# A transformer decoder block: cross attention and the stages before and after it, one after the other or in one order of gaps

## The chip, the cores and the metric

One core of one Trainium2 chip runs the program. The metric is the device time of one execution in microseconds (us), the median of several runs. The profile is one execution of the kernel before, recorded by the hardware profiler.

## The reference

A decoder block in float32: 4 batches of 1024 tokens, width 256, 16 heads of 16, a context of 154 tokens per batch, a feed-forward width of 1024. Cut to what is computed:

```python
nx = _ln(x, ln1_scale, ln1_bias)
q, k, v = heads(nx @ W_qkv)
x = x + merge(_attend(q, k, v, causal)) @ W_self_out
nx = _ln(x, ln2_scale, ln2_bias)
q = heads(nx @ W_q)
k, v = heads(encoder_output @ W_kv)
x = x + merge(_attend(q, k, v, None)) @ W_cross_out
nx = _ln(x, ln3_scale, ln3_bias)
return x + relu(nx @ W1 + b1) @ W2 + b2
```

## The kernel before, in words

The program is written engine by engine, each with its own fixed order; semaphores join them. SyncE (SP) issues every DMA, in one order. There are five stages, one behind the other.

- **A, the first stage** (`dense_a`): normalize x, q, k and v of self attention, and k and v of the context; parts go to DRAM.
- **SA, self attention** (`attention(SA, ...)`): 16 *windows*, v = 0 to 15. A window is four heads of one batch and has 12 *steps*: one block of 128 keys against a half of 512 queries (less on the diagonal). A step has four scores (`scores`, L765, TensorE (PE), 64 rows of the array in use), four exponentials (ScalarE (ACT), L1015) and the sum with the values (`weigh`, L784, array split in 32 columns). Before the scores of a window come the row maxima of its queries: `max_tile` (PE, L653) and VectorE's (DVE) reduction (L1123), two windows ahead; `turn` (L674), `negate` and `rows` put them as rows into the stack of queries.
- **C, the middle stage** (`dense_c`), for n = 0 to 7 (four batches times two halves of 512 tokens): `project_c` (output of self attention times W_self_out, L818), the sum with x, moments, normalize, `transposes` (L622), and the queries of cross attention (`project`, L627). The first n are begun in SA's last two windows (`ahead_c`), and the first maxima of XA run inside C.
- **XA, cross attention** (`attention(XA, ...)`): 16 windows of 4 steps, against 154 keys. Scores rotate over three banks, maxima over two pairs of banks; weights of the softmax have 16 slots in `probs`, and the sum is taken two steps behind the scores.
- **E, the last stage** (`dense_e`), for n = 0 to 7: `project_e` (W_cross_out), sum, moments, normalize, `transposes`, eight hidden tiles (the products of L635 to L637, bank to ReLU on ACT to a high part on DVE, L1349, to a low part on GpSimd (POOL), L1533), and the second product of the feed-forward. Every product there is three matmuls, high and low parts. In PE's order, `project_e` of the next n and its transposes stand between hidden tiles and result, and inside the result, of this one:

```python
for i in range(2):
    pe.wait_ge(y_done, 2 + 2 * n + i - 1)
    for t in range(2 * i, 2 * i + 2):
        ...
    last.then_inc(f_ready, 1)
    if i == 0 and (hf == 0 or more):
        transposes(E, n + 1, 1 - hf, 2)
```

Between the five scores' places of a step lies what else PE does: the lists `units_at`, `weigh_at` and `turn_at` of each `Attention` count these places (five to a step, `5 * s + i`). Call them *gaps*: 60 in a window of SA, 20 in one of XA. In SA's last two windows and in XA's, `ahead` adds the first steps of the stage that follows.

## Time and profile before

| | us |
|---|---|
| median of 3 runs | 1096.2 |
| runs | 1088.33 to 1098.66 |
| the profiled execution | 1099.86 |
| its span, first to last instruction | 1098.1 |
| PE busy | 1008.1 |
| DVE, ACT, POOL busy | 784.1, 612.4, 331.5 |
| mean granted clock of PE | 0.950 |

The span is what the trace covers; 1.8 us of the profiled execution lie around it. A granted clock of 1.00 is 2.4 GHz and of 0.50 is 1.2 GHz; a mean between them is a stretch with both.

### The profile page before, as it was taken

Reading aid. Unit: us, or ns where it says so; the run is one execution under the profiler, and the core shown is the slowest. Engines: PE = TensorE matmul, PEld = TensorE weight load, DVE = VectorE, ACT = ScalarE, POOL = GpSimd, SP = SyncE. Lnnn points to the kernel's source line nnn. Section 1 sums busy time; section 2 is a strip of 40 time slices with the busy share of each in tenths; the row PEclk is TensorE's granted clock in tenths of the full one; section 3 lists DMA queues with packets and bytes.
Section 4 is the critical chain, followed back from the end, with each engine's and each line's share of the span. In section 5 each row is a group of like instructions: output and inputs, shape, how many; then the busy total and the mean of one; then the engine's idle time right before and its main releaser. Section 6 shows DMA issues by size and latency. Waiting matters only on the chain.

```text
span 1098.1 us, 19967 instructions
## 1 busy us (share of the span) xinstructions
PE 1008.1 (92%) x7632; PEld 632.4 (58%) x7632; DVE 784.1 (71%) x1154; ACT 612.4 (56%) x1310; POOL 331.5 (30%) x516
## 2 busy tenths in 40 slices
PE   3968889999999999999999886999998899999997
PEld 3855655555555555555443553444443588888886
DVE  5746677999999999999422575788886855656561
ACT  4623327777777777777654222788887433323221
POOL 8311103323233222322332110011112554545453
PEclk9969999999999999999895997899999899999998
DMA  6885676353535444344015993444542111111100
GB/s 184 295 246 157 188 209 131 60 112 69 112 69 108 68 98 90 70 90 165 21 58 135 286 325 111 94 114 105 123 120 74 50 46 59 58 58 58 39 20 20
DMA packets 78639, 123.47 MB, mean 112 GB/s; under 512 B 11057, under 2 KB 52305, under 8 KB 73553
## 3 DMA queue, kind: packets, MB, share of 16 engines
q1 hardware_dynamic: 78544, 122.21, 43.0%
q8 instruction: 60, 0.98, 0.4%
q14 instruction: 35, 0.28, 0.1%
HBM read 71.96 MB, written 49.17 MB: 110 GB/s over the span
## 4 chain that ended last, share of the span: by engine, by line
PE 78%; DVE 11%; DMA 3%; issue 2%; POOL 2%; ACT 2%; SPq 2%; POOLq 0%; ACTq 0%; DVEq 0%
PE bank L784 18%; PE bank L765 17%; PE bank L653 11%; PE bank L635 8%; DVE mx L1123 8%; PE bank L636 7%; PE bank L637 7%; PE bank L818 2%; PE bank L661 2%; PE bank L627 2%; PE bank L622 1%; ACT probs L1015 1%; DMA vst_mem<-self_ctx 1%; DMA k_st<-k_parts 1%; SPq L417 1%
## 5 line engine op out<-in xcount | busy, mean ns | idle before, releaser
L1015 ACT ACTIVATE probs<-bank 128x512 f32<-128x512 f32 (+3 forms) x1024 | 457.2, 521 | 147.6 <-PE bank L765 141.9
L1123 DVE TENSOR_REDUCE mx<-bank 128x2 f32<-128x1024 f32 (+5 forms) x416 | 435.1, 1084 | 72.9 <-PE bank L653 35.4
L765 PE MATMUL bank<-q_st,k_st 64*128 64x512 f32 (+3 forms) x1024 | 302.3, 439 | 11.7 <-ACT probs L1015 7.5
L765 PEld LDWEIGHTS bank<-q_st,k_st 64*128 64x128 f32 x1024 | 141.9, 189 | 205.2 <-ACT probs L1015 179.6
L653 PE MATMUL bank<-k_st,q_st 62*128 62x154 f32 (+4 forms) x1280 | 229.0, 353 | 31.2 <-DVE mx L1123 20.1
L784 PE MATMUL bank<-probs,nx_mem 128*32 128x512 f32 (+3 forms) x2048 | 239.1, 545 | 0.2
L653 PEld LDWEIGHTS bank<-k_st,q_st 62*128 62x128 f32 x1280 | 145.9, 191 | 77.5 <-DVE mx L1123 58.3
L1454 POOL TENSOR_SCALAR_AFFINE_SELECT probs<-probs 128x256 f32<-128x256 f32 x256 | 103.9, 407 | 226.6 <-ACT probs L1015 226.3
L1533 POOL TENSOR_TENSOR hT_lo<-hT,hT_hi 128x512 fp32r<-128x512 f32 x64 | 93.1, 1475 | 91.9 <-DVE hT_hi L1349 91.9
L1463 POOL TENSOR_TENSOR oN<-oT,rs 128x256 f32<-128x256 f32 x64 | 40.6, 635 | 231.6 <-DVE rs L1207 231.6
L635 PE MATMUL bank<-nxT_lo,hT_hi 128*128 128x256 f32 x256 | 77.6, 303 | 17.7 <-issue 13.7
L936 ACT CAST probs<-bank 128x512 fp32r<-128x512 f32 x48 | 28.2, 587 | 106.1 <-PE bank L627 58.9
L1202 DVE STREAM_TRANSPOSE oT<-bank 128x512 f32<-128x512 f32 x64 | 45.7, 714 | 55.8 <-PE bank L784 55.4
L929 ACT ACTIVATE nxT<-bank,lnb_sb,lns_sb 128x512 f32<-128x512 f32 x48 | 35.0, 778 | 88.5 <-PE bank L622 88.5
L661 PE MATMUL bank<-below,eye 64*128 64x64 bf16 (+1 forms) x1024 | 82.7, 210 | 0.0
L1062 ACT ACTIVATE hT<-bank,b_sb 128x512 f32<-128x512 f32 x64 | 44.2, 690 | 68.8 <-PE bank L637 67.7
L1349 DVE CAST hT_hi<-hT 128x512 fp32r<-128x512 f32 x64 | 60.9, 965 | 26.8 <-ACT hT L1062 26.1
L636 PE MATMUL bank<-nxT_hi,hT_lo 128*128 128x256 f32 x256 | 76.1, 297 | 0.0
L637 PE MATMUL bank<-nxT_hi,hT_hi 128*128 128x256 f32 x256 | 76.0, 297 | 0.0
L784 PEld LDWEIGHTS bank<-probs,nx_mem 128*32 128x32 f32 x2048 | 42.6, 109 | 57.4 <-issue 37.1
L635 PEld LDWEIGHTS bank<-nxT_lo,hT_hi 128*128 128x128 f32 x256 | 53.0, 207 | 19.3 <-issue 19.3
L636 PEld LDWEIGHTS bank<-nxT_hi,hT_lo 128*128 128x128 f32 x256 | 53.2, 208 | 0.0
(119 smaller groups left out, 1260.6 us busy)
## 6 DMA issues: line engine op xcount, KB each, us to landing
xt<-in_x_dram SPq DMA_DIRECT2D x16, 512.0 KB, 5.9
q_parts<-probs SPq DMA_DIRECT2D x16, 512.0 KB, 6.7
k_parts<-probs SPq DMA_DIRECT2D x16, 512.0 KB, 4.0
q_st<-q_parts SPq DMA_DIRECT2D x32, 256.0 KB, 4.8
k_st<-k_parts SPq DMA_DIRECT2D x32, 256.0 KB, 6.6
qx_parts<-probs SPq DMA_DIRECT2D x16, 512.0 KB, 7.4
q_st<-qx_parts SPq DMA_DIRECT2D x32, 256.0 KB, 4.7
v_aug<-vst_mem SPq DMA_DIRECT2D x8, 544.0 KB, 4.4
```

Of the source, the lines that this page charges most:

```text
L635: pe.matmul(dst, a_hi, b_lo, start=(j == 0), stop=False)
L636: pe.matmul(dst, a_lo, b_hi, start=False, stop=False)
L637: last = pe.matmul(dst, a_hi, b_hi, start=False, stop=(j == len(terms) - 1))
L653: last = pe.matmul(banks[:, j, keys * y:keys * y + keys], q_st[w][h0:h0 + KROWS, i, P * qb:P * qb + P], keys_of(a, v0)[h0:h0 + KROWS, i, k ...
L661: last = pe.matmul(banks[:, j, end - width:end], eye[h0:h0 + HALF, e0:e0 + P], below[h0:h0 + HALF, 0:width], start=False, stop=width == HALF)
L765: pe.matmul(bank[:, m, 0:n], keys_of(a, v0)[rows, i // 2, P * kb:P * kb + P], q_st[w][rows, i // 2, lo:lo + n], start=True, stop=True).the ...
L784: last = pe.matmul(bank[32 * i:32 * i + 32, a.acc[hf % a.AB], lo - HF * hf:lo - HF * hf + n], v_cur[w // 2][:, col:col + 32], probs[:, pt, ...
L1015: act.activation(probs[:, use % NPT, 0:n], bank[:, a.s_banks[use % a.SB], 0:n], ACT.Exp, scale=SCALE).then_inc(a.exp_done, 1)
L1123: dve.tensor_reduce(mx[:, par, part].rearrange("p (j y) -> p j y", j=2)[:, :, blocks.start:blocks[-1] + 1:blocks.step], banks[:, :, 0:len( ...
L1349: dve.tensor_copy(hT_hi[:, f, :], hT[:, f % HRING, :]).then_inc(h_hi, 1)
L1454: pool.affine_select(out=tri, in_=tri, compare_op=ALU.is_ge, fill=0.0, base=0, pattern=[[0, 2], [1, P]], channel_multiplier=-1).then_inc(a ...
L1533: pool.tensor_tensor(hT_lo[:, f, :], hT[:, f % HRING, :], hT_hi[:, f, :].bitcast(F32), ALU.subtract).then_inc(h_lo, 1)
```

## The change

Stages C, XA and E are no longer one behind the other. One count of gaps runs through them, `at`, from -120 (SA's last two windows) over 0 to 319 (XA's 16 windows) to 418. Each engine walks the same count and does at each gap what the tables name: `C_PROJECT`, `C_TURN`, `C_PRODUCT` (gaps of each n), and for E the offsets `E_...` from `E_FROM[n]` = 101 + 40 n, so that one n of E takes two windows of XA. At a gap, PE does in this order: the sum of XA with its values (offset 3 of each step, now one step behind), `turn`, a unit of maxima, a score, and what stands `behind`: at most one piece of C or E.

So that all of it fits: every product of C and E goes through two banks in turn (`g_bank`, banks 6 and 7, ordered by `g_order`); XA keeps three score banks, has one accumulator as before, and one pair of banks for maxima in the place of two; XA's weights have 8 slots in the place of 16; its stacks of queries are three and not four, loaded in gap 1 of the window two before the one that uses them; its stacks of keys hold a whole batch and are two. The ring of hidden tiles before their split (`hT`) has two buffers, not four; the high part of a hidden tile is made by ACT, not by DVE; the weights of C and E are split by POOL in 9 pieces in windows 4 to 12 of SA, not by DVE and ACT before E. The rows of W1 and W2 are loaded in window 2 of SA. C's DRAM copy of x + attention and XA's queries remain DRAM round trips. The keys of the context are stored by four DMAs per batch in the place of two.

In the order of PE, between the transposes of an n of E (offset -3) and its first hidden tile (+1) lie four gaps; the hidden tiles stand at +1, +3 to +15, the result at +22, +24, +31 and +33, and `project_e` at -13 and -12.

```diff
+        probs_x, hT_hi = sb("probs_x", [P, NPT - FC, HF]), sb("hT_hi", [P, FC, HF], F32R)
...
+        late_st = sb("late_st", [P, 3, 2 * L], F32R)
+        q_st = [sb(f"q_st{w}", [P, 2, L], F32R) for w in range(3)] + [late_st[:, 1].rearrange("p (i t) -> p i t", i=2)]
+        k_st = [sb(f"k_st{w}", [P, 2, L], F32R) for w in range(2)] + [
+            late_st[:, w].rearrange("p (i t) -> p i t", i=2) for w in (0, 2)]
+        nxT_hi, nxT_lo = (late_st[:, w].rearrange("p (h k t) -> p h k t", h=2, k=KC) for w in (1, 2))
+        hT_lo = late_st[:, 0:2].rearrange("p a (f t) -> p (a f) t", t=HF)
+        cn_hi, cn_lo = (late_st[:, 2].rearrange("p (s k t) -> p s k t", s=2, k=KC)[:, i] for i in range(2))
+        wqx_sb = sb("wqx_sb", [P, KC, D])
...
+        w2_hi = sb("w2_hi", [P, FC, D], F32R)
+        parts_c = sb("parts_c", [P, 2, NPART, HF], F32R)
+        hT = [hT_0, sb("hT_1", [P, HF])]
...
-        XA = Attention("X", False, LX, 2, qx_parts, kx_parts, vx_aug, cross_ctx, [0, 1, 4], [5], [(2, 3), (6, 7)],
-                       units_at=(0, 8, 9, 11, 15, 17), turn_at=4, weigh_at=(1, 0, 3, 2),
-                       sums_at=(5, 1), invert_at=(5, 2), back_at=(6, 5), divide_at=(3, 1))
+        XA = Attention("X", False, LX, 2, qx_parts, kx_parts, vx_aug, cross_ctx, [0, 1, 2], [3], [(4, 5)], 1, NPT // 2, 3,
+                       units_at=(7, 9, 12, 14, 17, 19), turn_at=1, weigh_at=(3, 3, 3, 3),
+                       sums_at=(14, 4), invert_at=(15, 5), back_at=(18, 8), divide_at=(16, 6))
...
+        XG = 5 * XA.NS
+        X_END = 4 * B * XG
+        LAST_SELF = -2 * 5 * SA.NS
+        C_PROJECT = ((-115, -114), (-99, -98), (0, 1), (15, 16), (62, 63), (82, 83), (143, 145), (166, 170))
+        C_TURN = (-101, -85, 8, 23, 70, 92, 158, 180)
+        C_PRODUCT = ((-97, -96), (-81, -80), (11, 12), (26, 27), (73, 74), (94, 95), (160, 161), (183, 187))
+        C_LOAD = (None, None, -77, -65, 25, 72, 98, 160)
+        C_SUM, C_DEV, C_NORM, C_SCALE, C_HIGH, C_LOW, C_STORE = 1, 2, 4, 1, 1, 2, 3
+        E_FROM = tuple(5 * XG + 1 + 2 * XG * n for n in range(2 * B))
+        E_HIGH, E_LOW, E_PROJECT, E_SUM, E_DEV, E_BIAS, E_NORM = -16, -15, (-13, -12), (-12, -11), -10, -9, -7
+        E_TURN, E_SCALE, E_TOKENS, E_REST = -3, -2, -1, 0
+        E_FIRST, E_SECOND, E_ADD = (1, 3, 5, 7, 9, 11, 13, 15), (22, 24, 31, 33), (25, 34)
+        END = E_FROM[2 * B - 1] + E_ADD[1] + 3
+
+        EARLY_X = {**{-56 + 4 * n: (0, n) for n in range(XA.MT)}, **{-29 + 4 * n: (1, n) for n in range(XA.MT)}}
+        EARLY_TURN = -33
+
+        def e_at(n, r):
+            return E_FROM[n] + r
...
+        g_order = []
+        for at in range(LAST_SELF, END):
+            for n in range(2 * B):
+                g_order += [("C", "o", n, i) for i in range(2) if at == C_PROJECT[n][i]]
+                g_order += [("C", "t", n, k) for k in range(KC) if at == C_TURN[n]]
+                g_order += [("C", "q", n, c) for c in range(2) if at == C_PRODUCT[n][c]]
+            for n in range(2 * B):
+                g_order += [("E", "o", n, i) for i in range(2) if at == e_at(n, E_PROJECT[i])]
+                g_order += [("E", "t", n, k) for k in range(KC) if at == e_at(n, E_TURN)]
+                g_order += [("E", "h", n, f) for f in range(FC) if at == e_at(n, E_FIRST[f])]
+                g_order += [("E", "y", n, i) for i in range(2) if at == e_at(n, E_SECOND[2 * i])]
...
+        def g_bank(u):
+            return bank[:, 6 + u % 2, :]
...
+            for x_at in range(LAST_SELF, END):
+                v, g = divmod(x_at, XG)
...
+                if x_at in (-76, -75):
+                    w = x_at + 76
+                    sp.wait_ge(C.parts_stored[0], 16 * 2)
+                    load_stack(XA, "q", w)
+                if x_at == -50:
+                    sp.wait_ge(SA.st_ready, 4 * SA.NS * (4 * B - 1))
+                    sp.wait_ge(C.parts_stored[1], 16 * 2)
+                    load_stack(XA, "q", 2)
+                if x_at == -71:
+                    sp.wait_ge(v_spare, 1)
+                    load_values(XA, 0)
+                if x_at == 6:
+                    sp.wait_ge(v_spare, 2)
+                    load_values(XA, 2)
+                if x_at == EARLY_TURN + 3:
+                    rows(XA, 0)
+                if 0 <= v < 4 * B:
+                    if g == 1 and v and v + 2 < 4 * B:
+                        sp.wait_ge(XA.st_ready, 4 * XA.NS * v)
+                        sp.wait_ge(C.parts_stored[(v + 2) % 4 // 2], 16 * 2 * ((v + 2) // 4 + 1))
+                        load_stack(XA, "q", v + 2)
+                    if g == 2 and v % 4 == 0 and 0 < v < 4 * (B - 1):
+                        load_keys(v // 4 + 1)
+                    if g == XA.turn_at + 3 and v + 1 < 4 * B:
...
+                            sp.wait_ge(x1_stored[1], 16 * 2)
+                            sp.wait_ge(C.nx_ready, 4)
+                        sp.dma_start(xt[:, 1], tokens(x1_dram, b, hf)).then_inc(E.x_in[0], 16)
+                    if x_at == (4 * XG * (b + 1) + 3 if hf == 0 else e_at(n - 1, 2)):
+                        sp.wait_ge(XA.oC_stored[hf], 16 + 16 * (2 * b + 2))
...
+            def project_e(n, i):
+                u = g_use["E", "o", n, i]
+                pe.wait_ge(c_lo, n + 1)
+                pe.wait_ge(g_read[u % 2], u // 2)
+                for t in range(2 * i, 2 * i + 2):
+                    last = product(g_bank(u)[:, D * (t % 2):D * (t % 2) + D],
+                                   [(cn_hi[:, k, P * t:P * t + P], cn_lo[:, k, P * t:P * t + P], wco_hi[:, k, :],
+                                     wco_lo[:, k, :]) for k in range(KC)])
+                last.then_inc(g_ready[u % 2], 1)
...
+            def hidden_e(n, f):
+                u = g_use["E", "h", n, f]
+                pe.wait_ge(nxT_low, KC * n + KC)
+                pe.wait_ge(g_read[u % 2], u // 2)
+                product(g_bank(u), [(w1_hi[:, k, P * f:P * f + P], w1_lo[:, k, P * f:P * f + P],
...
+
+            def result_e(n, t):
+                u = g_use["E", "y", n, t // 2]
+                if t % 2 == 0:
+                    pe.wait_ge(g_read[u % 2], u // 2)
+                pe.wait_ge(h_lo, FC * n + FC)
+                last = product(g_bank(u)[:, D * (t % 2):D * (t % 2) + D],
+                               [(hT_hi[:, f, P * t:P * t + P], hT_lo[:, f, P * t:P * t + P], w2_hi[:, f, :], w2_lo[:, f, :])
+                                for f in range(FC)])
+                if t % 2:
+                    last.then_inc(g_ready[u % 2], 1)
...
+            def behind(at):
+                if at in EARLY_X:
+                    max_tile(XA, EARLY_X[at][0], 0, EARLY_X[at][1], XA.MB)
+                if at == EARLY_TURN:
+                    turn(XA, 0, 0, XA.MB)
+                for n in range(2 * B):
+                    for i in range(2):
+                        if at == C_PROJECT[n][i]:
+                            project_c(n, i)
+                    if at == C_TURN[n]:
+                        turn_tokens(C, "C", n, c_slot(n))
+                    for c in range(2):
+                        if at == C_PRODUCT[n][c]:
+                            product_c(n, c)
+                for n in range(2 * B):
+                    for i in range(2):
+                        if at == e_at(n, E_PROJECT[i]):
+                            project_e(n, i)
+                    if at == e_at(n, E_TURN):
+                        turn_tokens(E, "E", n, 1)
+                    for f in range(FC):
+                        if at == e_at(n, E_FIRST[f]):
+                            hidden_e(n, f)
+                    for t in range(TT):
+                        if at == e_at(n, E_SECOND[t]):
+                            result_e(n, t)
...
+                        pe.wait_ge(w_ordered, 2 * 2 * KC)
+                    if 4 * B - 2 <= v < 4 * B:
+                        behind(LAST_SELF + 5 * (q - (4 * B - 2) * SA.NS) + i)
 
...
+            for at in range(END):
+                v, g = divmod(at, XG)
+                if at == 5 + XA.weigh_at[0]:
+                    pe.wait_ge(SA.acc_free, 2 + 2 * 4 * B)
+                    pe.wait_ge(w_low, 9)
+                s = at // 5 - XA.LAG
+                if 0 <= s < 4 * B * XA.NS and at % 5 == XA.weigh_at[s % XA.NS]:
+                    weigh(XA, s // XA.NS, s % XA.NS)
+                if g == XA.turn_at and v + 1 < 4 * B:
+                    turn(XA, v + 1, 0, XA.MB)
+                for n in range(XA.MT):
+                    if g == XA.units_at[n] and v + 2 < 4 * B:
+                        max_tile(XA, v + 2, 0, n, XA.MB)
+                if v < 4 * B and g % 5 < 4:
+                    scores(XA, v, g // 5, g % 5)
+                behind(at)
 
 
...
+            def hidden(n, f):
+                u = g_use["E", "h", n, f]
+                if FC * n + f > 1:
+                    act.wait_ge(h_lo, FC * n + f - 1)
+                act.wait_ge(g_ready[u % 2], u // 2 + 1)
+                act.activation(hT[f % 2][:, :], g_bank(u), ACT.Relu, bias=b1_sb[:, f:f + 1]).then_inc(g_read[u % 2], 1)
+
+            def hidden_high(n, f):
+                u = g_use["E", "h", n, f]
+                act.wait_ge(g_read[u % 2], u // 2 + 1)
+                act.copy(hT_hi[:, f, :], hT[f % 2][:, :]).then_inc(h_hi, 1)
...
+            for at in range(END):
+                v, g = divmod(at, XG)
+                behind(at)
+                if v < 4 * B and g % 5 < 4:
+                    weight(XA, v, g // 5, g % 5)
...
+
+            def weights_rest(k):
+                raw, hi, lo = piece(k)
+                pool.wait_ge(w_high, k + 1)
+                pool.tensor_tensor(lo, raw, hi.bitcast(F32), ALU.subtract).then_inc(w_low, 1)
+
...
+            def hidden_low(n, f):
+                pool.wait_ge(h_hi, FC * n + f + 1)
+                pool.tensor_tensor(hT_lo[:, f, :], hT[f % 2][:, :], hT_hi[:, f, :].bitcast(F32), ALU.subtract).then_inc(h_lo, 1)
```

## Rows read from the trace of the kernel before

**Rows 1.** Busy time by stretch: window, then each engine's busy time, clock, DMA.

```profile
core 0: us, PE busy (x) PEld busy (x) DVE busy (x) ACT busy (x) POOL busy (x), PEclk, DMA share, GB/s
171.00:533.00 362.00, 360.73 (x3572) 186.10 (x3576) 333.92 (x390) 283.30 (x674) 107.41 (x252) 1.00 0.44 90
...
533.00:565.00 32.00, 30.12 (x155) 13.27 (x158) 4.70 (x13) 17.91 (x45) 10.87 (x29) 0.84 0.21 67
565.00:601.00 36.00, 34.07 (x175) 13.40 (x164) 8.14 (x22) 19.39 (x48) 10.35 (x23) 0.67 0.40 96
...
620.00:688.00 68.00, 56.39 (x240) 35.60 (x242) 40.41 (x87) 17.29 (x29) 5.18 (x10) 0.86 0.75 240
...
700.00:821.00 121.00, 118.14 (x976) 56.88 (x972) 102.92 (x156) 100.15 (x192) 14.89 (x24) 1.00 0.49 109
...
868.00:1076.00 208.00, 194.20 (x1248) 178.61 (x1246) 129.18 (x193) 62.47 (x94) 111.46 (x81) 0.97 0.15 46
1076.00:1098.10 22.10, 14.10 (x96) 13.92 (x96) 1.99 (x3) 0.67 (x1) 3.65 (x3) 0.85 0.07 24
```

**Rows 2.** The chain that ended last, in order of time, around stage C.

```profile
609.41 10.78 DMA vst_mem<-self_ctx
...
625.63 3.43 PE bank L627 x8
629.94 3.46 PE bank L818 x16
```

**Rows 3.** Groups of instructions by form in 700 to 820 us.

```profile
L653 PEld LDWEIGHTS bank<-k_st,q_st 62*128 62x128 f32 x384 | 36.0, 186 | 15.3 <-DVE mx L1123 14.8
```

**Rows 4.** Timeline of PE inside XA: start, us, instruction.

```profile
753.36 0.49 PE L765 MATMUL bank<-q_st,k_st 64*128 64x512 f32 x2
...
753.78 1.07 PE L784 MATMUL bank<-probs,nx_mem 128*32 128x512 f32 x8
...
754.77 0.50 PE L765 MATMUL bank<-q_st,k_st 64*128 64x512 f32 x1
```

**Rows 5.** Timeline of PE: a product of E (12 matmuls) between scores of XA.

```profile
840.04 0.51 PE L765 MATMUL bank<-q_st,k_st 64*128 64x512 f32 x2
840.48 0.39 PE L635 MATMUL bank<-wco_lo,cT_hi 128*128 128x256 f32 x1
...
841.90 0.28 PE L637 MATMUL bank<-wco_hi,cT_hi 128*128 128x256 f32 x1
842.11 0.49 PE L765 MATMUL bank<-q_st,k_st 64*128 64x512 f32 x1
```

**Rows 6.** Timeline of PE in E, from 256-column to 512-column matmuls.

```profile
920.75 0.28 PE L637 MATMUL bank<-nxT_hi,hT_hi 128*128 128x256 f32 x1
920.87 0.40 PE L635 MATMUL bank<-nT_lo,w_hi 128*128 128x512 f32 x1
...
921.34 0.39 PE L637 MATMUL bank<-nT_hi,w_hi 128*128 128x512 f32 x1
921.57 0.40 PE L635 MATMUL bank<-nT_lo,w_hi 128*128 128x512 f32 x1
```

**Rows 7.** Timeline of the steps behind the transposes of E's first n.

```profile
856.77 1.45 ACT L929 ACTIVATE nxT<-bank,lnb_sb,lns_sb 128x512 f32<-128x512 f32 x2
...
858.75 1.29 DVE L1318 TENSOR_TENSOR nT_lo<-nxT,nT_hi 128x512 fp32r<-128x512 f32 x2 [1.18 <-ACT nT_hi L1054]
```

**Rows 8.** Groups of instructions by form on POOL in 868 to 1076 us.

```profile
L1533 POOL TENSOR_TENSOR hT_lo<-hT,hT_hi 128x512 fp32r<-128x512 f32 x60 | 87.7, 1480 | 88.5 <-DVE hT_hi L1349 88.5
```

**Rows 9.** Timeline of SP: the issue of one stack of queries.

```profile
747.34 2.42 SPq L417 DMA_DIRECT2D q_st<-qx_parts  x4
```

**Rows 10.** DMA issues by line: KB each, median us to landing.

```profile
q_st<-qx_parts SPq DMA_DIRECT2D x32, 128.0 KB, 4.8
cross_ctx<-oC SPq DMA_DIRECT2D x16, 256.0 KB, 2.0
...
vst_mem<-cross_ctx SPq DMA_DIRECT2D x8, 512.0 KB, 3.8
```

More of the change, by code:

```diff
@@ new lines, in project_c @@
+            def project_c(n, i):
+                u, z = g_use["C", "o", n, i], c_slot(n)
+                pe.wait_ge(C.x_in[z], 32 * (c_slot_use(n) + 1))
+                if u > 1:
+                    pe.wait_ge(g_read[u % 2], u // 2)
+                for t in range(2 * i, 2 * i + 2):
+                    for k in range(KC):
+                        last = pe.matmul(g_bank(u)[:, D * (t % 2):D * (t % 2) + D], cT[:, z, k, P * t:P * t + P],
+                                         wso_sb[:, k, :], start=(k == 0), stop=(k == KC - 1))
+                last.then_inc(g_ready[u % 2], 1)
@@ L1544 @@
+            for at in range(END):
+                v, g = divmod(at, XG)
+                for hf in range(2):
+                    if g == XA.divide_at[hf] and 0 <= v - hf < 4 * B:
+                        divide(XA, v - hf, hf)
+                behind(at)
 _PRE = "L0_xattn_"
```

1195 lines of the change are left out of this document (544 added, 651 removed).

## The prediction

> **What bounds the kernel now.** I read the busy time by stretch first, because the stages have different limits. In self attention PE is busy 360.7 of 362.0 us at full clock, 14 windows of 25.9 us [rows 1]; the change leaves that part alone, and its windows 14 and 15 begin at about 533 us. What follows is 565 us, and that is what the change is about. There the reader is to see four different kinds of loss. Windows 14 and 15 have no maxima left to do, PE waits for exponentials, and the granted clock falls to 0.84 and then 0.67, so part of it runs at 1.2 GHz [rows 1]. Stage C starts with a load of 10.8 us on the chain that ended last, and in 68 us behind that PE is busy 56.4 at a clock of 0.86, with the DMA engines at 0.75 [rows 1, 2]. Cross attention is 121 us for 12 windows, 10.1 us each, PE 118 and ACT 100 busy [rows 1]: it looks like an ACT stage, but PE has next to nothing free. The last stage is PE's again: 194 of 208 us [rows 1], 29.2 us for an n.
>
> So the gain can only be the time in which PE waits or is slow, and the question is what PE's own list of work costs when the pieces are mixed.
>
> **Prices on PE, full clock.** A 512-column matmul of the last stage takes 0.23 us start to start ((921.57 - 920.87) / 3), a 256-column one 0.12 [rows 6]. Hidden tiles are 48 of the first (10.9 us), the result 96 of the second (11.5), `project_e` 24 (2.9), the transposes 8 of about 0.11 (0.9, an estimate: half of 0.23): 26.2 us for an n. An n of C is 16 matmuls of `project_c` (3.5), 8 of the queries (3.4) [rows 2] and the transposes: 7.8 us. A sum with the values takes 0.99 us (754.77 - 753.78), a pair of scores in front of it 0.42 [rows 4]. A window of cross attention with maxima has 10.1 us less waits. PE's modelled idle time is 0.24 us of it (2.9 / 12) [rows 1], and weight loads for maxima wait 15.3 / 12 = 1.3 us for DVE, partly under running matmuls [rows 3]; I take 9.4, between 9.8 and 8.5. Without maxima it is 4 x 0.99 + 8 x about 0.33 = 6.6 (a pair between 0.23 and 0.42). A self window without maxima: sums 8.9, scores 7.5, both scaled with the columns; part of each does not shrink with them, so I take 17 us, against 283.3 / 14 = 20.2 of exponentials [rows 1].
>
> **What mixing adds on PE.** Inside cross attention the trace already has one product of the full array between scores: from the pair at 840.04 to the next score at 842.11 are 2.07 us, of which 0.23 + 12 x 0.12 = 1.67 are streaming [rows 5]. So 0.40 us go into the two changes of shape. Back to back, the pair in front of a sum shows the same: 0.42 for 0.23 of columns [rows 4]. Where a block stands beside a sum, one of the changes is paid already. I take 0.28 per block, with ends 0.15 and 0.40. The Trainium skill (TensorEngine Tiling (Array Packing), Key Properties) says that changing the tiling mode, not just the tile, drains TensorE; the trace agrees. The rule speaks against this change, which turns one run of full-array matmuls into blocks of 6 or 24 between scores of 64 rows; without it the sum below would be 31 us lower. An n of E has 15 blocks (8 hidden, 4 results, 2 projections, 1 pair of transposes), one of C 5 (1.4 us, so 9.2 for an n). Scores that lose their partner cost about 1 us more per n of E.
>
> **What it takes away elsewhere.** The ReLU's high part leaves DVE for ACT: eight casts for an n. In two windows ACT then has 2 x 8.35 us of exponentials [rows 1] and some 13 of E's, 30 of 50: it hides. The low part on POOL is 1.48 us a tile [rows 8], 11.8 an n, under 18 us of hidden tiles mixed with XA. One pair of maxima banks makes PE wait for each reduction before the next unit, and everything behind the unit in PE's order waits too. Two or three gaps lie between two units; where a block or a sum stands in them I cost the wait at nothing. Its bounds are 0 and, uncovered, twice the 1.3 us a window of now [rows 3]. POOL's splitting of weights lies in SA's windows where POOL is busy 107 of 362 us [rows 1]: nothing. SP waits at gap 80 (b + 1) + 3 for the landing of a store (2.0 us [rows 10]); queued behind it are the rows of the next window, which have 16 gaps left, and at other gaps loads of x: nothing, unless several such waits follow each other (the second rival).
>
> **The sum**, by four parts.
> - SA's last two windows (120 gaps), now with n = 0 and 1 of C and 12 early maxima: window 14 is 17 + 2 x 9.2 = 35.4; window 15 is 17 + 12 x 0.55 = 23.6 (0.55, an estimate, six matmuls and their loads), above ACT's 20.2. 59 us, all at full clock, since PE no longer waits. Before, it was 68.
> - Gaps 0 to 100: five windows of cross attention. With little between them they keep 10.1: 50.5. C's n = 2 to 5: 36.8. `project_e` and transposes of the first E: 4.6. Waits 10: the chain sum, moments, deviation, normalize between `C_PROJECT` and `C_TURN` for n = 2 and 3, about 5; queries loaded at gap 1 and needed at gap 7, where four issues and the landing are 2.4 + 4.8 = 7.2 us [rows 9, 10] against 3 or 4 us of PE in the one bare window, 3; the first `c_in`, 2. Together 102.
> - Gaps 101 to 320: windows 5 to 13 are 84.6, 14 and 15 are 13.2; E is five n and the first part of a sixth, 142; 83 blocks x 0.28 = 23; lost pairs 5; C's n = 6 and 7, 18.4. Waits, 2.5 us for each of 5.5 n, 14: scaled, high and low part take 3.3 us from the transposes to the first hidden tile (856.77 to 860.04) [rows 7], the four gaps between hold about 1.5, and the rest is the store and load of `c_in` (2.0 + 3.8 and their issue [rows 10]) for even n. Together 300.
> - Behind the last score: results of n = 5, two projections and transposes, hidden tiles and results of two n: 11.5 + 5.8 + 1.8 + 44.8 = 64, and one sum, 1. Here nothing covers the chains any more: 3.3 us twice in front of the hidden tiles, where before the transposes lay in the middle of the result; the wait between hidden tiles and result, and the end, 22.1 - 14.1 = 8.0 for the last n [rows 1] and about 4 for the one before; `c_in` of n = 6, stored at gap 319 and needed at 328, 4; the ring of two, where ReLU, cast and low part must end before the third tile, 2. Together 90.
>
> 533 + 59 + 102 + 300 + 90 = 1084, plus the 1.8 outside the span: 1086 against 1099.9 for the profiled execution, 14 us or 1.3% less. That execution lies 3.7 above the median of the runs; against 1096.2 the forecast is **1082**. Of the 565 us, PE's list without mixing is about 462 (56 + 86 + 255 + 65, the four parts without blocks, lost pairs and waits). Before, 103 us of loss stood on it; after, 89, of which 37 are new (113 blocks at 0.28 and 5 for pairs).
>
> **Rivals.**
> - *The price of a block decides, nothing is left over.* At 0.40 per block, 83 + 30 blocks cost 14 us more: 1096, the median of now. For it: the only block of its kind in the trace costs 0.40 [rows 5]. Against it: about a third of the new blocks touch a sum.
> - *Slower: the one order couples engines through leads that are too short.* Queries reach the stack 7.2 us after SP's turn at gap 1 [rows 9, 10], and the maxima at gap 7 are in PE's queue before everything else of E and C; SP itself comes late when it waits for a landing in front. With the single maxima pair and one step of lag, a wait then stops scores, exponentials and products alike. If each of windows 1 to 13 loses 2.5 us more than I gave it, the time is 1082 + 33 = 1115. It decides from the point at which the first seven gaps hold under 7.2 us of PE work: bare they hold 3 to 4, with three hidden tiles about 8, with two results 9. So the cover is thin, by less than 1 us in odd windows. POOL's low part and ACT's order can do the same to the two product banks.
> - *Better: waits hide.* With blocks at 0.15 and half of the 24 us of waits that I gave outside the end, 1082 - 15 - 12 = 1055. For it: ACT's and DVE's chains were measured where nothing ran beside them.
> - *The change does not do what it says*, E stays behind XA because a wait holds the count back: then C's gain alone is left, about 1080 to 1096; I hold this for unlikely, the order is fixed in PE's program.
>
> **How the numbers follow.** A measurement of this kernel can tell about 1% from no change (runs span 0.9%). Forecast and better case 0.44 for faster by over 1% (under 1085); the block price and smaller errors around it 0.25 for within 1%; coupling 0.31 for slower. The range runs from 1045 (under the better case, since the clock may hold everywhere) to 1122 (above the coupling case). As cases of both signs hold much of the chance: the forecast's own range is 1068 to 1095.
>
> **What would show it.** In the profile after: no stretch between 535 and 600 us with a clock under 0.9; windows 14 and 15 of SA at 25 to 35 us; score to score over a hidden tile about 0.3 us above 1.36 plus columns; two windows of cross attention with an n of E in 52 to 54 us (before, 20.1 + 29.2 = 49.3 apart): mixing E with XA costs, and all the gain comes from C and SA's end. PE waits in front of the first hidden tile for DVE, 1.5 to 2 us each time, and behind the last score 3 us. Wrong would make it: PE waiting for DVE's reduction or for the load of queries in most windows; a block at 0.1 us; ACT, with casts and ReLU in its order, holding the scores back.

## The result and the profile after

The changed kernel takes **1169.8 us** (median of 4 runs, 1167.2 to 1181.0) against 1095.9 for the kernel before in the same session: 1.071 times as long, interval 1.062 to 1.079. The forecast was 1082 with a range to 1122. The profiled execution has a span of 1169.1 us and a mean granted clock of 0.944 (before 1098.1 and 0.950).

The busy time by stretch, cut at the borders of the prediction's four parts: self attention up to window 14, windows 14 and 15, gaps 0 to 100, gaps 101 to 320, behind the last score. It answers to [rows 1].

```profile
core 0: us, PE busy (x) PEld busy (x) DVE busy (x) ACT busy (x) POOL busy (x), PEclk, DMA share, GB/s
172.00:531.00 359.00, 357.94 (x3544) 184.84 (x3544) 332.54 (x386) 280.07 (x667) 124.06 (x275) 1.00 0.44 91
531.00:579.20 48.20, 42.74 (x209) 20.79 (x208) 15.05 (x39) 25.17 (x56) 11.46 (x25) 0.89 0.49 138
579.20:615.10 35.90, 30.03 (x226) 14.69 (x227) 15.51 (x20) 20.34 (x49) 8.10 (x19) 0.86 0.46 98
615.10:754.70 139.60, 113.94 (x560) 57.53 (x560) 72.69 (x147) 57.85 (x102) 14.63 (x22) 0.80 0.39 109
754.70:1072.00 317.30, 299.31 (x1814) 190.78 (x1814) 139.64 (x256) 172.96 (x306) 93.66 (x89) 0.97 0.31 80
1072.00:1169.10 97.10, 72.83 (x456) 64.22 (x456) 23.57 (x43) 28.34 (x43) 29.50 (x24) 0.91 0.11 36
```

Each row splits into three: PE idle (length less busy), time lost to the half clock (half of PE's busy time that lies where the trace's record of the granted clock stands at 0.50), and the rest, which is **PE's work at full clock**. The loss is taken on busy time alone; on the whole length, an idle microsecond at half clock would be counted as idle and as slow. Busy x (1 - clock), summed over rows of 4 us of the same view, gives it to 1 us (44.4 and 39.9 us for the kernel after and before). The rest can be held against the prediction's list of work without its waits.

| part | length, forecast | length | idle, forecast | idle | half clock | work, forecast | work |
|---|---|---|---|---|---|---|---|
| windows 14, 15 | 59 | 84.1 | 0 | 11.3 | 7.5 | 59 | 65.2 |
| gaps 0 to 100 | 102 | 139.6 | 10 | 25.7 | 23.0 | 92 | 91.0 |
| gaps 101 to 320 | 300 | 317.3 | 14 | 18.0 | 8.2 | 286 | 291.1 |
| behind the last score | 90 | 97.1 | 25 | 24.3 | 6.1 | 65 | 66.7 |
| together | 551 | 638.1 | 49 | 79 | 45 | 502 | 514 |

Of the 87 us too many, 45 are half clock, which the forecast had at nothing, 30 are waits, nearly all of them in the first two parts, and 12 are work. The same split of the kernel before and after, over everything behind window 13 of self attention, one row each:

```profile
533.00:1098.10 565.10, 515.87 (x3239) 347.25 (x3238) 340.32 (x568) 263.31 (x482) 171.55 (x185) 0.92 0.35 96
```

```profile
531.00:1169.10 638.10, 558.86 (x3264) 348.00 (x3263) 266.46 (x503) 304.65 (x552) 157.35 (x178) 0.91 0.32 85
```

Before: 49 idle, 41 half clock, 475 work. After: 79, 45, 514. So the change adds 39 us of work, 30 of idle time and 4 of half clock. The prediction had put 40 us of work on top of its list for mixing, so this part of it held. What the change was to recover, 90 us of idle and slow time, became 124.

Where PE waits. First the chain that ended last, at three places; a row is start, duration, what. It answers to [rows 2].

```profile
573.42 0.90 SPq L550
...
576.21 7.90 DMA q_st<-qx_parts
584.11 0.04 issue
584.16 0.92 PE bank L718 x3
...
725.00 8.38 DMA vst_mem<-cross_ctx
...
845.10 0.58 SPq L471
...
846.25 11.00 DMA vst_mem<-cross_ctx
857.25 0.02 issue
857.28 1.05 ACT late_st L1083
858.33 0.02 issue
858.35 1.24 DVE late_st L1302
```

The first is inside window 15 of self attention: the early maxima of cross attention (L718) stand in PE's order before the scores behind them, and their queries have only just been stored and read back. The second and third are `c_in`, the attention's output for `project_e` of even n. SP issues four loads of queries and four of keys (both L471, 0.6 us each, the last of keys shown at 845.10) right in front of it, and the landing takes 8.4 and 11.0 us where the kernel before had a median of 3.8 [rows 10].

Then the groups of PE's instructions by form, with the idle time before them, in gaps 0 to 100:

```profile
L826 PE MATMUL bank<-q_st,k_st 64*128 64x512 f32 x82 | 35.0, 554 | 6.2 <-ACT probs_x L1064 6.2
L718 PE MATMUL bank<-k_st,q_st 62*128 62x154 f32 x160 | 21.4, 329 | 11.5 <-DMA q_st<-qx_parts 5.8 <-DVE mx L1183 5.7
L867 PE MATMUL bank<-ident,vst_mem 128*128 128x128 f32 x40 | 6.7, 321 | 3.3 <-DVE vst_mem L1169 3.3
L739 PE MATMUL bank<-ident,mx 128*32 128x128 f32 x6 | 1.9, 320 | 3.9 <-DVE mx L1183 3.9
```

and behind the last score:

```profile
L695 PE MATMUL bank<-w_lo,hT_hi 128*128 128x256 f32 x96 | 27.2, 283 | 5.8 <-POOL late_st L1534 5.8
L695 PE MATMUL bank<-late_st,w_hi 128*128 128x512 f32 x32 | 14.7, 459 | 5.5 <-DVE late_st L1307 5.5
L695 PE MATMUL bank<-wco_lo,late_st 128*128 128x256 f32 x16 | 5.5, 341 | 4.0 <-DVE late_st L1302 4.0
L867 PE MATMUL bank<-ident,vst_mem 128*128 128x128 f32 x16 | 2.5, 287 | 4.1 <-DVE vst_mem L1169 4.1
```

No single wait is long: from 531 us on PE waits 38 times for 0.5 us or more, 67 us together, and the longest is 5.7. Each is at the end of a short chain between engines. The first row of the windows shows self attention untouched: PE busy 357.9 of 359.0 us at full clock.

### The profile page after: what moved, and what is told of

The parts are those of the page before. It is cut to its first block, busy times and chain, and to the rows that moved or that the text cites. A ratio compares the mean times of both kernels' runs of the same rounds, so it can differ in the third digit from the quotient of the medians.

```text
span 1169.1 us, 20136 instructions
## 1 busy us (share of the span) xinstructions
PE 1047.7 (90%) x7632; PEld 631.3 (54%) x7632; DVE 709.0 (61%) x1085; ACT 650.3 (56%) x1373; POOL 334.4 (29%) x532
## 4 chain that ended last, share of the span: by engine, by line
PE 71%; DVE 13%; DMA 5%; ACT 3%; SPq 2%; issue 2%; POOL 2%; POOLq 0%; DVEq 0%; ACTq 0%
PE bank L826 16%; PE bank L845 16%; PE bank L718 10%; PE bank L695 8%; DVE mx L1183 7%; PE bank L697 6%; PE bank L696 6%; PE bank L877 3%; PE bank L857 3%; DMA vst_mem<-cross_ctx 2%; PE bank L726 2%; DMA q_st<-qx_parts 2%; SPq L471 2%; PE bank L867 1%; DVE stats L1158 1%
## 5 line engine op out<-in xcount | busy, mean ns | idle before, releaser
L1064 ACT ACTIVATE probs<-bank 128x512 f32<-128x512 f32 (+3 forms) x768 | 323.8, 494 | 108.9 <-PE bank L826 103.9
L1064 ACT ACTIVATE probs_x<-bank 128x512 f32<-128x512 f32 x256 | 144.4, 598 | 142.4 <-PE bank L826 141.6
L826 PE MATMUL bank<-q_st,k_st 64*128 64x512 f32 (+3 forms) x640 | 209.5, 451 | 8.9 <-ACT probs_x L1064 7.4
L718 PE MATMUL bank<-k_st,q_st 62*128 62x154 f32 (+4 forms) x896 | 146.5, 345 | 38.3 <-DVE mx L1183 17.6
L845 PE MATMUL bank<-probs,nx_mem 128*32 128x512 f32 (+3 forms) x1536 | 162.1, 501 | 0.6 <-POOL probs L1485 0.5
L718 PEld LDWEIGHTS bank<-k_st,q_st 62*128 62x128 f32 x896 | 95.4, 197 | 72.5 <-DVE mx L1183 35.3
L1534 POOL TENSOR_TENSOR late_st<-hT,hT_hi 128x512 fp32r<-128x512 f32 x64 | 82.0, 1281 | 140.2 <-ACT hT_hi L1101 138.8
L695 PE MATMUL bank<-w_lo,hT_hi 128*128 128x256 f32 x256 | 74.4, 291 | 5.8 <-POOL late_st L1534 5.8
L845 PE MATMUL bank<-probs_x,nx_mem 128*32 128x512 f32 x512 | 74.1, 653 | 0.7 <-ACT probs_x L1064 0.7
L697 PE MATMUL bank<-w_hi,hT_hi 128*128 128x256 f32 x256 | 71.9, 281 | 0.0
L696 PE MATMUL bank<-w_hi,late_st 128*128 128x256 f32 x256 | 71.7, 280 | 0.0
L1314 DVE TENSOR_TENSOR xn<-xn,bank 128x512 f32<-128x512 f32 x16 | 10.9, 682 | 84.5 <-PE bank L697 84.5
```

The lines of the kernel that those rows point to most:

```text
L695: pe.matmul(dst, a_hi, b_lo, start=(j == 0), stop=False)
L696: pe.matmul(dst, a_lo, b_hi, start=False, stop=False)
L697: last = pe.matmul(dst, a_hi, b_hi, start=False, stop=(j == len(terms) - 1))
L718: last = pe.matmul(banks[:, j, keys * y:keys * y + keys], queries_of(a, v0)[h0:h0 + KROWS, i, P * qb:P * qb + P], keys_of(a, v0)[h0:h0 + K ...
L826: pe.matmul(bank[:, m, 0:n], keys_of(a, v)[rows, i // 2, P * kb:P * kb + P], queries_of(a, v)[rows, i // 2, lo:lo + n], start=True, stop=T ...
L845: last = pe.matmul(bank[32 * i:32 * i + 32, a.acc[hf % a.AB], lo - HF * hf:lo - HF * hf + n], v_cur[w // 2][:, col:col + 32], a.probs[:, p ...
```

## The experiments

Effects are differences of the ratios to the kernel before, whose median in these sessions was 1087.4 to 1092.2 us; 0.01 is 11 us. The intervals are +-0.003 to 0.009, so a difference from the changed kernel is known to about 10 us. Single traces differ too: window 15 of self attention runs the same code in the changed kernel and in experiments 3, 4, 5, 7, 9 and 14, and takes 36 to 43 us in their traces, at a granted clock of 0.62 to 0.86. Only a difference in the stretch that an edit touches, or one clearly over 10 us, counts below.

**1. One place for maxima in the kernel before.** It was part of the change and I had costed it at nothing.

```diff
-        XA = Attention(... [0, 1, 4], [5], [(2, 3), (6, 7)],
+        XA = Attention(... [0, 1, 4], [5], [(2, 3)],
```

> The kernel before with one pair of banks (2, 3) for cross attention's maxima in the place of two; all tables unchanged. If the loss comes from waits of PE on single resources in nearly bare windows (theory of waits), the 14 windows with maxima lose 2 to 4 us each and the clock falls with them: 1096 + 30 to 60. If it comes from the changes of shape (theory of blocks), this costs under 10 us.

Measured 1156.8 us, ratio 1.066 (1.060 to 1.072): +72 us, as much as the whole change. PE's groups in its cross attention, 732 to 842 us, and its cross attention from the first exponential to the last, above the same of the kernel before:

```profile
L653 PE MATMUL bank<-k_st,q_st 62*128 62x154 f32 x224 | 29.1, 325 | 19.3 <-DVE mx L1123 19.3
```

```profile
671.70:913.50 241.80, 200.58 (x1237) 85.97 (x1237) 140.50 (x208) 137.60 (x257) 23.01 (x33) 0.81 0.31 73
```

```profile
684.60:856.20 171.60, 164.12 (x1234) 76.74 (x1234) 135.65 (x208) 134.30 (x256) 23.00 (x33) 0.95 0.44 103
```

By the split that is 41 us idle against 7 and 42 of half clock against 8: the waits cost 34 us, and the clock that fell with them 33 more. Windows take 13.1 us where the clock is full and 15 to 19.5 where it is not, against 10.1. This looked like the whole answer. The next runs show that it is not: here only scores stand between the units at gaps 8, 9 and 11, in the changed kernel a block or a sum mostly does.

**2 to 4. The three waits that the profile after names, one by one.** Shorter reductions (16 of 154 keys), no loads of queries from window 3 on (and no wait of PE for them), and `c_in` of even n loaded nine gaps earlier, from other data and without waiting for a store.

```diff
-  ...rearrange("p j (y k) -> p j y k", k=keys), AX.X, ALU.max
+  ...rearrange("p j (y k) -> p j y k", k=keys)[:, :, :, 0:keys if a.causal else 16], AX.X, ALU.max
```

> The changed kernel; DVE's reduction for cross attention reads 16 of the 154 keys, so that the single pair comes free about 0.9 us sooner (the subtracted value is then the maximum over 16 keys only). Theory of waits: 20 to 35 us less than 1170, most of it in windows 0 to 4 of cross attention. Theory of blocks: under 8 us less.

```diff
-                        load_stack(XA, "q", v + 2)
+                        if v == 0:
+                            load_stack(XA, "q", v + 2)
```

> The changed kernel without the loads of queries for windows 3 to 15 of cross attention and without PE's waits for them (these windows use the stacks of the first three). Theory of waits: the lead of six gaps costs the 10 us of PE's wait and as much in half clock: 12 to 20 us less. Theory of blocks: nothing.

```diff
-                    if x_at == (4 * XG * (b + 1) + 3 if hf == 0 else e_at(n - 1, 2)):
+                    if x_at == (4 * XG * (b + 1) - 6 if hf == 0 else e_at(n - 1, 2)):
...
-                        load_attended(cross_ctx, c_in, b, hf, 1)
+                        load_attended(cross_ctx if hf else self_ctx, c_in, b, hf, 1)
```

> The changed kernel; for even n of the last stage the attended tile is loaded nine gaps earlier and from the self-attention array, so that it waits for no store (the data are other data of the same size). Theory of waits: ACT waited 27.8 us for four of these loads, with PE's scores behind it: 15 to 25 us less. Theory of blocks: nothing.

Measured 1153.9 (ratio 1.061, 1.058 to 1.064), 1157.3 (1.063, 1.059 to 1.067) and 1162.5 us (1.069, 1.062 to 1.077): 10, 9 and 1 us less than the changed kernel's 1.071. Each acts just where its theory puts it (windows from first exponential to first exponential). Reductions: windows 0 to 2 of cross attention 25.6, 18.5, 21.9 us for 30.1, 24.1, 23.4 (window 0, which neither of the other two edits touches, takes 26.9 and 31.0 in their traces, so that of its difference little is sure). Queries: window 2, which holds next to nothing else, 12.9 for 23.4. `c_in`: window 4, 29.1 for 35.0, of which the windows behind give part back (5: 30.5 for 27.2). None is large, and none of the three totals stands clearly outside the error of 10 us.

**5. Fewer, longer blocks.** Hidden tiles and results of E in pairs, 9 blocks for an n in the place of 15.

```diff
-        E_FIRST, E_SECOND, E_ADD = (1, 3, 5, 7, 9, 11, 13, 15), (22, 24, 31, 33), (25, 34)
+        E_FIRST, E_SECOND, E_ADD = (1, 1, 5, 5, 9, 9, 13, 13), (22, 22, 31, 31), (24, 33)
```

> The changed kernel; hidden tiles stand in pairs at gaps 1, 5, 9, 13 and the four pieces of the result in pairs at 22 and 31, so that an n of the last stage has 9 blocks and not 15. Theory of blocks, at 0.28 to 0.4 us for a block: 9 to 13 us less over the 5.5 n that run beside cross attention, more if a block costs more. Theory of waits: no gain, or a loss, since the two product banks and the exponentials wait for longer blocks.

Measured 1193.0 us, 1.090 (1.081 to 1.099): 20 us more.

```profile
530.00:1191.30 661.30, 568.58 (x3264) 364.77 (x3264) 261.40 (x505) 300.95 (x554) 156.67 (x178) 0.88 0.31 82
```

By the split: idle 93, half clock 65, work 504. The work did fall, by 10 us; behind the last score it is the same (66.5 us for 66.7), so the 34 blocks less beside cross attention gave it, 0.3 us a block. So the price of a block was right, and the theory that blocks made up the miss is wrong: taking them away saves 10 us of work and adds 13 of waits and 20 of half clock. The Trainium skill (TensorEngine Tiling (Array Packing), Key Properties) says that a change of tiling mode drains TensorE; the measured 0.3 us a block agree with it.

**6. Experiments 2, 3 and 4 together.**

> The changed kernel with the three edits of short maxima, no query loads and early context together (16 of 154 keys in the maxima, old queries in windows 3 to 15, other data in the attended tiles of even n). Theory of waits: 50 to 80 us less than 1170, and a granted clock in windows 0 to 4 of cross attention of over 0.9 in the place of 0.80. Theory of blocks: under 20 us less.

Measured 1132.6 us, 1.040 (1.032 to 1.048): 34 us less than the changed kernel, where 50 to 80 were expected. The three alone add up to 20; the 14 between are within the error of such a sum. Gaps 0 to 100, and the whole from window 14 on:

```profile
614.80:725.60 110.80, 98.58 (x560) 51.14 (x560) 51.76 (x147) 56.51 (x102) 15.62 (x22) 0.94 0.35 111
```

```profile
531.30:1132.20 600.90, 540.89 (x3264) 340.72 (x3264) 196.11 (x505) 303.74 (x553) 158.56 (x178) 0.95 0.24 73
```

Idle 60, half clock 25, work 516. Gaps 0 to 100 fall from 139.6 to 110.8 us, and there the clock rises from 0.80 to 0.94: 13 us less idle and 16 less of half clock at the same work, 92 us for 91. In all, 19 us less idle time brought 19 less of half clock. Even so the kernel is 4% slower than before. It lies 36 us above the 565 of before, and that is the work: 516 against 475, with idle and half clock together at 85 against 90.

**7 and 8. The clock by itself.** In the changed kernel identity matmuls fill waits of the last two n; in the kernel before, doubled scores fill self attention's last two windows.

```diff
+            def fill(at):
...
+                for n in (6, 7):
+                    for r, many in ((E_PROJECT[0], 8), (E_TURN, 8), (E_FIRST[0], 12), (E_SECOND[0], 12)):
+                        if at == e_at(n, r):
+                            for _ in range(many):
+                                pe.matmul(bank[:, 0, 0:P], ident[:, :], ident[:, :], start=True, stop=True)
```

> The changed kernel with extra matmuls of the identity into a free bank in PE's order, 8 or 12 of them in front of the four places of n = 6 and 7 of the last stage where PE waits 2 to 3 us behind the last score. They take PE time only while it waits. Theory that the half clock is the price of the waits: the clock behind the last score rises from 0.91 to over 0.95 and 3 to 6 us are won. If waits alone cost: no difference, or 1 to 3 us lost.

```diff
+                        if a is SA and (4 * B - 2) * a.NS + 4 <= q < 4 * B * a.NS and i == 3:
+                            ...
+                            for j in range(2):
...
+                                pe.matmul(bank[:, 6 + j, 0:n], keys_of(a, v0)[rows, 1, P * kb:P * kb + P],
+                                          q_st[w][rows, 1, lo:lo + n], start=True, stop=True)
```

> The kernel before with two extra score matmuls (results unused, a free pair of banks) behind the fourth score of each step in the last two windows of self attention from its fifth step. If the half clock there comes from PE's thin work, the clock rises from 0.84 and 0.67 to over 0.95 and the two windows take 55 to 60 us instead of 68: 8 to 12 us less than before. If ACT sets the pace there, nothing changes or 2 us are lost.

From the last exponential to the end, the changed kernel and then experiment 7:

```profile
1071.90:1169.10 97.20, 72.83 (x456) 64.22 (x456) 23.57 (x43) 28.44 (x43) 29.59 (x24) 0.91 0.11 36
```

```profile
1073.80:1165.70 91.90, 85.32 (x616) 78.09 (x616) 23.57 (x43) 28.43 (x43) 29.63 (x24) 0.99 0.12 38
```

The last two windows of self attention in experiment 8, and below them in the kernel of experiment 1, which is the same as the kernel before in these windows and has no filling:

```profile
529.00:564.00 35.00, 32.48 (x224) 15.55 (x222) 8.24 (x23) 23.16 (x58) 13.49 (x34) 1.00 0.19 62
564.00:600.00 36.00, 34.38 (x210) 19.20 (x211) 15.03 (x40) 19.33 (x45) 10.49 (x21) 1.00 0.65 134
```

```profile
530.00:560.00 30.00, 28.01 (x171) 12.70 (x170) 6.23 (x17) 20.00 (x49) 12.20 (x31) 1.00 0.22 72
560.00:600.00 40.00, 36.78 (x223) 19.48 (x224) 16.65 (x44) 23.27 (x54) 12.25 (x25) 1.00 0.56 125
```

The kernels measure 1163.4 us (1.070, 1.061 to 1.078) and 1089.4 (1.000, 0.996 to 1.004): neither total can be told from its kernel without filling. The traces tell more. In the changed kernel the clock behind the last exponential rises from 0.91 to 0.99 and the stretch falls from 97.2 to 91.9 us, 5.3 less, where experiments 2, 3, 4, 6 and 11 have 97.0 to 97.6 with the same code. So there the half clock is a price of the waits and filling them wins it back, as expected; the total is too coarse to show 5 us.

Experiment 8 can't be read in the same way. The clock of the two windows is 1.00 with the filling, but it is 1.00 in the trace of experiment 1 without it too. Those windows (first exponential of window 14 to last of window 15) take 57.3 us with filling and 56.2 without, and 68.0 in the trace that the prediction rests on, where the clock had fallen to 0.84 and 0.67 [rows 1]. That is what the half clock costs there, 11 to 12 us, and it comes in some executions and not in others: in 32 executions of the kernel before beside these experiments the time falls by about 9 us for each 0.01 more of the mean granted clock, from 1098 at 0.953 to 1085 at 0.970. The ten with filling lie on the same line (0.959 to 0.970). Whether filling keeps the clock up there is not shown.

**9 and 10. Maxima packed closer, then E eight gaps later as well.** Units at gaps 11, 12, 14, 16, 17, 19 give the queries 4 more gaps to land; E_FROM = 109 + 40 n gives `c_in` 8 more.

```diff
-                       units_at=(7, 9, 12, 14, 17, 19), turn_at=1, weigh_at=(3, 3, 3, 3),
+                       units_at=(11, 12, 14, 16, 17, 19), turn_at=1, weigh_at=(3, 3, 3, 3),
```

> The changed kernel with cross attention's units of maxima at gaps 11, 12, 14, 16, 17, 19 instead of 7, 9, 12, 14, 17, 19, so that the queries have ten gaps from their load. Theory of waits: the window with nearly nothing beside it (v = 2, 23.4 us) falls to about 16 and the time by 5 to 12 us, less what the closer units lose to the single pair.

> As the one before, and every n of the last stage eight gaps later (E_FROM 109 + 40 n), so that the attended tile of even n has ten gaps from its load and not two. Theory of waits: windows 4, 8 and 12 lose their extra 5 to 10 us each, the end comes 8 gaps later (3 to 5 us): 10 to 20 us less than 1170 in all.

Measured 1220.3 (1.122, 1.113 to 1.131) and 1218.7 us (1.118, 1.109 to 1.127): over 50 us more, where less was expected. PE's units of maxima in 700 to 1100 us of the first of them:

```profile
L718 PE MATMUL bank<-k_st,q_st 62*128 62x154 f32 x352 | 42.8, 298 | 27.3 <-DVE mx L1183 27.3
```

Units side by side on one place stop PE, as in the first experiment; spread out they do so much less (5.7 us in the changed kernel's 615 to 1060 us).

**11 to 13. The number of places in the changed kernel.** Eight banks leave no room for a second pair. So the units are made narrow enough for one bank (80 keys, one half of the rows), and the same unit runs with one bank or two in turn; the last adds the edits of 3 and 4.

```diff
+        NARROW = 80
...
+                            dst = bank[:, 4 + a.tile_use(v0, n) % ring, NARROW * (3 * j + y):NARROW * (3 * j + y) + NARROW]
...
-        XA = Attention(... [0, 1, 2], [3], [(4, 5)], 1, NPT // 2, 3,
+        XA = Attention(... [0, 1, 2], [3], [(4, 5), (4, 5)], 1, NPT // 2, 3,     # in 12 and 13 alone
```

> The changed kernel with narrower units of maxima in cross attention: six matmuls of 80 keys, all on the upper rows, into one bank (480 columns), in the place of three pairs of 154 keys into a pair of banks. It leaves out 74 of 154 keys and half of the heads from the maxima. One place for units as in the changed kernel; it is the control of the next kernel, which differs in the number of places alone. PE's streaming is about the same (6 x 80 against 3 x 154 columns), DVE's reduction half as long. From the kernel with short reductions (1153.9): 1150 to 1160 by every theory.

> As the control before it, but units take turns between two banks. Theory that the one place for maxima is the main cause (one pair alone cost the kernel before 61 us): 30 to 60 us below the control, 1095 to 1125, and windows 0 to 2 of cross attention at 18 us or less. Rival that the count of gaps loses its time through other waits (queries, c_in, the two product banks) and the place hardly matters here, because C's and E's blocks already lie between units: within 10 us of the control.

> As the kernel before it with two places, and also no loads of queries from window 3 on and the load of c_in for even n early and from the output of self attention (other data, as in the two experiments of these alone; 80 of 154 keys in the maxima). If the three causes add up: the two-place kernel less 15 to 20 us; 1080 to 1110 by the theory of the one place, 1130 by the rival. Gaps 0 to 100 at 95 to 105 us, which the prediction forecast with 102.

Measured 1202.5 (1.103, 1.097 to 1.109), 1197.9 (1.098, 1.093 to 1.102) and 1171.7 us (1.074, 1.069 to 1.080). The control was to be at 1150 to 1160 and is over 40 above; the last section has the part of it that the traces explain. The units are the same in all three, so the comparison between them stands. The same group in 615 to 1060 us, with one place and with two:

```profile
L726 PE MATMUL bank<-k_st,q_st 62*128 62x80 f32 x462 | 74.9, 303 | 9.9 <-DMA q_st<-qx_parts 7.6 <-DVE mx L1195 2.4
```

```profile
L726 PE MATMUL bank<-k_st,q_st 62*128 62x80 f32 x462 | 72.7, 298 | 7.6 <-DMA q_st<-qx_parts 7.6
```

The second place removes PE's wait for the reduction to the last tenth, and is worth 4.6 us, 0.005 of the ratio and inside the intervals. My theory after the first experiment, that the single place is the main cause, falls. Its share lies between that and the 10 us of the second experiment. Taking away queries and `c_in` as well saves 26 us more.

**14. E eight gaps later, nothing else.**

```diff
-        E_FROM = tuple(5 * XG + 1 + 2 * XG * n for n in range(2 * B))
+        E_FROM = tuple(5 * XG + 9 + 2 * XG * n for n in range(2 * B))
```

> The changed kernel with the last stage eight gaps later for every n (E_FROM = 109 + 40 n), nothing else. If the load of c_in comes too late for project_e (the chain holds vst_mem <- cross_ctx with 8.4 and 11.0 us), windows 4, 8 and 12 fall from 35, 39 and 29 us to 29, 31 and 25, about 20 us in all, against 8 gaps more behind the last score at 0.8 us, 6 us: 1155. Rival, the wait moves to the next thing that is late (the maxima's pair, VectorE): windows as before and 1170 to 1178.

Measured 1197.9 us, 1.097 (1.092 to 1.103): 29 us more. The late load is gone: ACT waited 27.8 us for `c_in` in four places in the changed kernel, and waits for it no more. But now PE waits more for DVE, 15.6 us in front of hidden tiles (9.9 in the changed kernel) and 16.3 for the low part of `c_in` (0.5 there):

```profile
L695 PE MATMUL bank<-late_st,w_hi 128*128 128x512 f32 x90 | 42.1, 468 | 16.2 <-DVE late_st L1307 15.6 <-ACT nxT L1071 0.5
L695 PE MATMUL bank<-wco_lo,late_st 128*128 128x256 f32 x40 | 15.5, 389 | 16.3 <-DVE late_st L1302 16.3
```

One such wait in the timeline of DVE (PE waits from about 873.5 to 878.1 us):

```profile
873.33 1.12 DVE L1183 TENSOR_REDUCE mx<-bank 128x6 f32<-128x924 f32 x1 [4.09 <-PE bank L718]
874.36 0.71 DVE L1260 STREAM_TRANSPOSE oT<-bank 128x512 f32<-128x512 f32 x1
874.99 1.34 DVE L1169 TENSOR_SCALAR vst_mem<-xt,mv,rstd 128x256 f32<-128x256 f32 x4
876.25 0.68 DVE L1314 TENSOR_TENSOR xn<-xn,bank 128x512 f32<-128x512 f32 x1
876.84 1.22 DVE L1302 TENSOR_TENSOR late_st<-vst_mem,late_st 128x1024 fp32r<-128x1024 f32 x1
```

and of ACT at the same place:

```profile
868.88 1.04 ACT L1083 CAST late_st<-vst_mem 128x1024 fp32r<-128x1024 f32 x1
```

The high part of `c_in` is there at 869.9. DVE is idle for 4.1 us, but its next instruction in the count of gaps is a reduction of a unit that PE reaches only at 872.7. The low part stands four places behind it and begins at 876.8, and PE, which is at `project_e`, waits for it. Both engines wait for each other in turns, each with work that it could do: **one count for all engines lets none run ahead**. The trace shows it at this place; that it is behind the waits of the changed kernel in general is argued from it and was not tried, for instance by another order on DVE.

## Why the prediction was wrong, step by step

- **"59 us, all at full clock, since PE no longer waits"** is the step that failed, and with it every part, since all were priced at full clock. I reasoned that C's work would fill PE in windows 14 and 15. But it fills PE with chains: transposes wait for the normalization (3.4 us), early maxima for the queries just stored (3.2 us, the chain at 576) and for reductions (1.0), scores for exponentials (2.6). PE's work there is 65.2 us for 59; idle time of 11.3 and a loss of 7.5 at a clock of 0.89 and 0.86 are the rest of 84.1. Over the four parts the half clock is 45 us against none in the forecast. The kernel before has 41: a gain that I counted in full did not come.
- **"Waits 10"** for gaps 0 to 100 is the second failed step: it measured 25.7, and 23.0 of half clock with them. C's chain has 3.3 for the 5 that I gave. The queries have 5.8 for 3, and window 2 is indeed the bare one (12.9 us without the load, 23.4 with it). There the load took what I had summed, from the first issue at 669.5 to the last landing at 676.6, 7.1 us for 7.2, but PE ran out of work 2.4 us behind the issue and not 3 to 4. `c_in` had 2 us for the first, but four issues of queries and four of keys in front and the landing of 8.4 us made it 6. The largest term I had at nothing: PE waits 9.6 us for DVE's reductions, 5.7 before the next unit and 3.9 before the turn behind the last.
- **"I cost the wait at nothing"** for the single place of maxima, where a block or sum stands between, was too low, but not by much: 5 to 10 us in all by experiments 2 and 12, neither clear of the error. Uncovered it costs 72 (experiment 1). The bound that I gave, twice the 1.3 us of a window, 36 in the 14 windows, holds for the idle time alone (34); the half clock that came with it doubled it.
- **PE's list** was nearly right: 502 us forecast, 514 measured. What mixing adds was right, 40 us forecast and 39 measured, blocks at 0.28 forecast and 0.3 measured; the list under it was too low from the start, 462 for the 475 of the kernel before. A part of that are the hidden tiles (48 at 0.233 us are 11.2 and not 10.9). The "113 blocks" and "37 new" leave out 10 blocks of C that are in the sum; with them they are 123 and 40. Otherwise, "two windows with an n of E in 52 to 54": 53.2 and 53.7 where no C lies between. So was the wait in front of E's first hidden tile (1.5 to 2 forecast, 9.9 / 6 = 1.65 measured) and the tail: idle 24.3 for 25.
- **The rivals.** Coupling through short leads was the right one, with the queries in the bare window as its place. Its price, 2.5 us for each of 13 windows, is 33 us, as much as the idle time that came out too long (30); the 45 us of clock come on top. That rival should have been the forecast: the prediction itself had found cover thin "by less than 1 us".

What stays open: experiment 6 leaves 60 us idle and 25 slow, and of the idle time 21 waits of 1 to 4 us are 46; no run took these apart. Why the idle time costs as much again in clock at some places and nothing at others was not measured either. That the loss in windows 14 and 15 comes from the early maxima and the normalization is read from the waits; it was not tried on its own.

## What to carry to other kernels

Split every stretch into idle, half clock and work at full clock before you price a new order: the new order adds work (here 39 us, most of it changes of shape), and it can only win from the other two. Take the half clock on busy time alone. Price a wait with the clock that it may cost: the half clock that came with more idle time was a tenth of it (before to after), as much (experiments 1 and 6) or one and a half times as much (experiment 5). Don't count on a full clock unless PE is seen to be busy without gaps through the whole stretch, and look at the clock of more than one execution of the kernel before: here 12 of the 90 us that the change was to recover were in its profile and not in that of experiment 1. When several in-order engines walk one count, look for places where engine X's next instruction needs Y and Y's next needs X; a longer lead did not help there. A different order on X might; that was not tried.

## What was not expected of the hardware

- The landing of a DMA goes with what was issued just in front: `c_in` (512 KB) has a median of 3.8 us before [rows 10]. In the changed kernel it takes 3.6 us with one store in front, 6.4 behind four loads of queries, 8.4 and 11.0 behind four of queries and four of keys, and 11.3 behind another 512 KB and four of queries. Without the loads of queries (experiment 3) the last four figures are 4.4, 6.2, 9.1 and 7.0.
- Six maxima matmuls of 62 rows, three for each half of the rows, take 0.56 us (x6, 154 columns); six on one half take 0.86, though they have half the columns:

```profile
861.24 0.56 PE L718 MATMUL bank<-k_st,q_st 62*128 62x154 f32 x6
```

```profile
851.92 0.86 PE L726 MATMUL bank<-k_st,q_st 62*128 62x80 f32 x6
```

The overlap of the two halves of the array is worth more than the columns. The work by the split grew by 19 us with these units (533 for 514). That explains under half of the 49 us by which the control of experiment 11 is slower than the kernel of experiment 2; the rest is half clock (66 us for 33), and why the clock fell so far was not measured.
